# Keys once a tile, loop limits a step ahead, the count flag behind the maxima, two scrap rows and rotated banks in a graph network kernel

## The reference

```
# block 1: attention, residual
h   = layernorm(x) @ W1                       # 4 heads of 192
e   = leaky_relu(s_src[src] + s_dst[dst]); a = softmax of e over the edges of each dst
o1  = sum over edges of a * h[src] + b1       # then the same again with W2, 2 heads of 96 -> o2
x1  = layernorm(x + concat(x, o2) @ Wu + bu)
# block 2: graph convolution, residual
norm = deg^-0.5[src] * deg^-0.5[dst]          # self-loops included
y   = relu(segsum((x1 @ V1)[src] * norm) + c1)
out = layernorm(x1 + segsum((y @ V2)[src] * norm) + c2)
```

## Time and profile before

| | us |
|---|---|
| median of 3 runs | 895.5 |
| lowest, highest | 892.07, 897.51 |
| the profiled execution, device time | 891.93 |
| its span, first to last instruction | 890.2 |
| TensorE busy in it | 805.7 (91%) |
| VectorE busy | 612.3 (69%) |
| ScalarE busy | 287.3 (32%) |

### The profile page before, as it was taken

The page is one execution under the profiler, slowest core; times in us unless marked ns, Lnnn a source line. Parts: engine busy times, 40 slices in busy tenths (PEclk is TensorE's granted clock), DMA queues, the critical chain, the costliest instruction groups (busy, mean ns, idle before and its releaser), DMA issues.

```text
span 890.2 us, 12683 instructions
## 1 busy us (share of the span) xinstructions
PE 805.7 (91%) x4306; PEld 667.0 (75%) x4307; DVE 612.3 (69%) x1304; ACT 287.3 (32%) x523; POOL 18.7 (2%) x32
## 2 busy tenths in 40 slices
PE   4999999998899199999989879699998999999997
PEld 3845555655666099999955679478887888999997
DVE  1788888887738999999689799765641823212444
ACT  4334555543532143434232444322221411111000
POOL 3100000000000040000000000000000000000000
PEclk9999999999989699999989898799999999999999
DMA  8300000000000040110000400000003000000111
GB/s 290 138 1 1 1 0 0 0 0 1 1 0 1 7 172 1 60 60 1 1 1 0 134 1 1 2 1 1 1 0 126 1 1 1 1 1 1 54 71 50
DMA packets 9573, 26.34 MB, mean 30 GB/s; under 512 B 623, under 2 KB 2477, under 8 KB 9138
## 3 DMA queue, kind: packets, MB, share of 16 engines
q1 hardware_dynamic: 9522, 25.65, 8.3%
HBM read 21.78 MB, written 3.87 MB: 29 GB/s over the span
## 4 chain that ended last, share of the span: by engine, by line
PE 66%; DVE 19%; issue 5%; DVEq 5%; ACT 3%; DMA 1%; SPq 0%
PE ps L1059 63%; DVE scrap L510 5%; DVE att L662 3%; DVEq L319 3%; DVE att L626 3%; DVE ohs_abc L521 1%; DMA w<-in_L_gnn_W 1%; DVEq L521 1%; DVE ohd_ab L524 1%; DVE ohd_c L524 1%; PE ps L1198 1%; DVE xohd L524 1%; DVE out L649 1%; DVE gw1lo L702 1%; PE ps L1339 1%
## 5 line engine op out<-in xcount | busy, mean ns | idle before, releaser
L1059 PE MATMUL ps<-g,att 128*128 128x193 f32 x800 | 133.2, 330 | 19.8 <-DVE att L626 19.8
L1059 PEld LDWEIGHTS ps<-g,att 128*128 128x128 f32 x800 | 132.3, 192 | 20.8 <-issue 20.4
L931 ACT ACTIVATE att<-att,ssrc 128x1250 f32<-128x1250 f32 x60 | 80.2, 1338 | 116.1 <-DVE att L662 116.0
L626 DVE SCALAR_TENSOR_TENSOR att<-att,ct 128x1250 f32<-128x1250 f32 x60 | 88.0, 1467 | 4.8 <-ACT att L931 4.6
L662 DVE SCALAR_TENSOR_TENSOR att<-uB,s 128x1250 f32<-128x1250 f32 x60 | 91.1, 1522 | 0.0
L1059 PE MATMUL ps<-wp,xT 128*128 128x388 f32 x240 | 87.6, 503 | 0.9 <-ACT xT L878 0.6
L1059 PE MATMUL ps<-yhi,ctr 128*128 128x384 f32 x200 | 67.7, 339 | 0.0
L726 DVE SCALAR_TENSOR_TENSOR ylo_a<-ps,dinv,yhi 128x384 fp32r<-128x384 f32 x32 | 19.0, 615 | 61.9 <-ACT yhi L815 61.9
L1059 PEld LDWEIGHTS ps<-wp,xT 128*128 128x128 f32 x240 | 42.8, 191 | 24.6 <-issue 1.0
L1059 PE MATMUL ps<-h2x,att 128*128 128x97 f32 x400 | 51.8, 294 | 10.0 <-DVE out L649 4.6
L1059 PEld LDWEIGHTS ps<-h2x,att 128*128 128x128 f32 x400 | 50.4, 209 | 11.4 <-DVE att L626 8.0
(11 more groups left out here) (238 smaller groups left out, 1467.2 us busy)
## 6 DMA issues: line engine op xcount, KB each, us to landing
wux<-in_L_gnn_Wu SPq DMA_DIRECT2D x2, 2304.0 KB, 15.9
gw<-in_L_gnn_W SPq DMA_DIRECT2D x2, 2304.0 KB, 10.0
uB<-u_dram SPq DMA_DIRECT2D x3, 1280.0 KB, 5.9
xs<-in_x SPq DMA_DIRECT2D x1, 3456.0 KB
out<-ybuf SPq DMA_DIRECT2D x9, 384.0 KB, 2.3
w<-in_L_gnn_W SPq DMA_DIRECT2D x1, 2304.0 KB, 8.5
w2x<-in_L_gnn_W SPq DMA_DIRECT2D x1, 576.0 KB, 9.2
wuo<-in_L_gnn_Wu SPq DMA_DIRECT2D x1, 576.0 KB
```

What stands on the lines that cost most here:

```text
L626: v.scalar_tensor_tensor(a, a, HUGE, ct[:, q, 0:N], ALU.min, ALU.mult).then_inc(att_ready, 1)
L931: a.activation(at_, at_, ACT.Exp, bias=ssrc[:, h, q:q + 1]).then_inc(att_exp, 1)
L1059: return t.matmul(o, lhsT, rhs, start=start, stop=stop, **kw)
```

## The change

- **Key once a count tile.** `key` is made once a tile (relative to the tile's first column); three new tables vkey1, vkey2, vkey3, written once by POOL, hold the values of `vkey` moved by 32, 64 and 96, and window w compares with the w-th. The wait for the key stands once at the head of the tile.
- **Loop limits one step ahead.** The limits of a tile's first window are loaded at its head. Those of windows 1 to 3 are loaded during the window before: on VectorE `end` behind unit 0 and `unit0` behind unit 1, on TensorE `end` behind unit 1. `first` is the `end` of the window before and isn't loaded.
- **Two scrap rows.** Maxima write to two rows in turn and wait for the last but one.
- **Flag behind the maxima.** The 30 maxima of heads 1 to 3 stand ahead of the wait for `dmax_ps`, the flag and the reciprocals.
- **Rotated banks.** In layer 1 the five banks of a head rotate over seven (0 to 4, 6, 7); TensorE waits for a bank only from the eighth use on. Layer 2 stays with banks 0 to 4.

```diff
--- before.py
+++ after.py
@@ -166,6 +166,8 @@
         ssB_a = at("ssB_a", [P, H1 - 1, NP], F32, R_WP)
         ssB_d = at("ssB_d", [P, NP], F32, R_G)
         scrap1 = at("scrap1", [P, NP], BF16, R_WP + 15360)
+        scrap1b = at("scrap1b", [P, NP], BF16, R_T1 + 7680)
+        scrap2b = at("scrap2b", [P, NP], BF16, R_G + 14400)
         uRow = at("uRow", [VR, P], F32R, R_T1 + 12800)
         uLine = at("uLine", [2 * T, P], F32, R_T1 + 12800)
         o2T = at("o2T", [P, 2, H2, P], F32, R_WP + 9472)
@@ -180,6 +182,9 @@
         ohd_ab = at("ohd_ab", [P, 2, PR, WC, 2], BF16, R_T1 + 5120)
         xohd = at("xohd", [P, 2, PR, WC, 2], BF16, R_T1 + 10240)
         ohd_d = at("ohd_d", [P, PR, WC, 2], BF16, R_MASK + (T - 1) * NP * 2)
+        vkey1 = at("vkey1", [P, WC, 2], I16, R_T1 + 7680)
+        vkey2 = at("vkey2", [P, WC, 2], I16, R_T1 + 8960)
+        vkey3 = at("vkey3", [P, WC, 2], I16, R_T1 + 1536)
         sRow = at("sRow", [VR, P], F32R, R_T1 + 12288)
         h2x = at("h2x", [P, T, H2, C2 + 1], F32, R_T1)
         x1Thi = at("x1Thi", [P, KD, P], F32R, R_T1 + 6144)
@@ -273,6 +278,7 @@
         win_ps, win_out = sem("win_ps"), sem("win_out")
         ct_out = sem("ct_out")
         wu_plus = sem("wu_plus")
+        vkeys_set = sem("vkeys_set")
         xh_ready = sem("xh_ready")
         svec_hi = sem("svec_hi")
         tp_ps, tp_out = sem("tp_ps"), sem("tp_out")
@@ -340,6 +346,9 @@
         def src_row(hp):
 
             return ([ssB_a[:, h, :] for h in range(H1 - 1)] + [ssB_b[:, :], ssB_c[:, :], ssB_d[:, :]])[hp]
+
+        def acc_bank(hp, b):
+            return (0, 1, 2, 3, 4, 6, 7)[(5 * hp + b) % 7] if hp < H1 else b
 
         def wide_counts(eng):
 
@@ -426,6 +435,9 @@
             step(pool.iota(iota[:, :, :], pattern=[[1, P], [0, 2]], base=0, channel_multiplier=0, **io))
             pool.iota(wcol[:, :], pattern=[[W, NW]], base=0, channel_multiplier=0, **io).then_inc(const_a, 1)
 
+            pool.wait_ge(const_a, 1)
+            for w, table in enumerate((vkey1, vkey2, vkey3)):
+                pool.iota(table[:, :, :], pattern=[[NP, T], [1, W], [0, 2]], base=W * (w + 1), channel_multiplier=0, **io).then_inc(vkeys_set, 1)
             for wu, loaded in ((wux, wux_in), (wux2, wux2_in)):
                 pool.wait_ge(loaded, 16)
                 for k in range(KD):
@@ -505,47 +517,52 @@
 
             def maximum(h, q, done):
 
-                if done > 0:
-                    v.wait_ge(mx_done, done)
-                v.tensor_tensor_reduce(out=(scrap1 if h < H1 else scrap)[:, 0:N], in0=src_row(h)[:, 0:N], in1=mask[:, q, 0:N], scale=1.0, scalar=-FAR,
+                if done > 1:
+                    v.wait_ge(mx_done, done - 1)
+                place = ((scrap1, scrap1b) if h < H1 else (scrap, scrap2b))[done % 2]
+                v.tensor_tensor_reduce(out=place[:, 0:N], in0=src_row(h)[:, 0:N], in1=mask[:, q, 0:N], scale=1.0, scalar=-FAR,
                                        op0=ALU.subtract, op1=ALU.max, accum_out=mx[:, h % H1, q:q + 1]).then_inc(mx_done, 1)
 
-            def window(q, w):
+            def one_hots(p0, src_hot, dst_hot, vk, kv, done):
+                v.tensor_tensor(src_hot, iota[:, None, :, :].to_broadcast([P, PR, P, 2]), sloT[:, bass.ds(p0, PR), None, :].to_broadcast([P, PR, P, 2]), ALU.is_equal)
+                v.tensor_tensor(dst_hot, vk[:, None, :, :].to_broadcast([P, PR, WC, 2]), kv[:, bass.ds(p0, PR), None, :].to_broadcast([P, PR, WC, 2]), ALU.is_equal).then_inc(done, 1)
+
+            def window(q, r, w, limits):
+
                 win = WPT * q + w
-                first, end, unit0 = window_range(v, win, 0, 1, 2)
-
-                kv = key[:, w % 2, :, :].rearrange("p a c -> p (a c)")
-                v.tensor_scalar(kv, keyT[:, :, :].rearrange("p a c -> p (a c)"), wcol[:, bass.ds(win, 1)], None, ALU.subtract).then_inc(v_own, 1)
-
-                def one_hots(p0, src_hot, dst_hot, done):
-                    v.tensor_tensor(src_hot, iota[:, None, :, :].to_broadcast([P, PR, P, 2]), sloT[:, bass.ds(p0, PR), None, :].to_broadcast([P, PR, P, 2]), ALU.is_equal)
-                    if done is unit_ready:
-                        v.wait_ge(v_own, V0 + win + 1)
-                    v.tensor_tensor(dst_hot, vkey[:, None, :, :].to_broadcast([P, PR, WC, 2]), key[:, w % 2, bass.ds(p0, PR), None, :].to_broadcast([P, PR, WC, 2]), ALU.is_equal).then_inc(done, 1)
-
+                first, end, unit0 = limits
+                vk, kv = (vkey, vkey1, vkey2, vkey3)[w], key[:, r, :, :]
+                nxt = [end]
                 for j in range(UW):
                     slot = (UW * w + j) % RING
                     v.wait_ge(unit_used, UW * win + j + 1)
                     p0 = nc.s_assert_within(v.snap((unit0 + j) * PR), 0, (UN - 1) * PR,
                                             skip_runtime_bounds_check_because="the first unit was clamped")
-                    one_hots(p0, ring_src(slot), ring_dst(slot), unit_ready)
+                    one_hots(p0, ring_src(slot), ring_dst(slot), vk, kv, unit_ready)
+                    if w + 1 < WPT and j < 2:
+                        nxt += window_range(v, win + 1, j + 1)
                 with v.Fori(first, end) as n:
                     p0 = nc.s_assert_within(v.snap((unit0 + UW + n - first) * PR), 0, (UN - 1) * PR,
                                             skip_runtime_bounds_check_because="the range was clamped to the units")
                     place = v.snap(n % 2)
                     v.wait_ge(extra_used, n + 1)
-                    one_hots(p0, xohs[:, bass.ds(place, 1), :, :, :].rearrange("p a b v c -> p (a b) v c"), xohd[:, bass.ds(place, 1), :, :, :].rearrange("p a b v c -> p (a b) v c"), extra_ready)
-
-
-            def tile(q, behind, last):
-
-                window(q, 0)
+                    one_hots(p0, xohs[:, bass.ds(place, 1), :, :, :].rearrange("p a b v c -> p (a b) v c"), xohd[:, bass.ds(place, 1), :, :, :].rearrange("p a b v c -> p (a b) v c"),
+                             vk, kv, extra_ready)
+                return nxt
+
+            def tile(q, r, behind, last):
+
+                limits = window_range(v, WPT * q, 0, 1, 2)
+                v.tensor_scalar(key[:, r, :, :].rearrange("p a c -> p (a c)"), keyT[:, :, :].rearrange("p a c -> p (a c)"), wcol[:, bass.ds(WPT * q, 1)], None,
+                                ALU.subtract).then_inc(v_own, 1)
+                v.wait_ge(v_own, V0 + q + 1)
+                limits = window(q, r, 0, limits)
                 if behind:
                     dense_out(q - 1, 1)
-                window(q, 1)
+                limits = window(q, r, 1, limits)
                 if last:
                     dense_out(q, 0)
-                window(q, 2)
+                limits = window(q, r, 2, limits)
                 dense_out(q, 1 if last else 0)
                 if last:
                     v.wait_ge(dn_out, 2 * T + 2)
@@ -553,18 +570,19 @@
                     v.tensor_copy(svec[:, 0:H1 * T], a4).then_inc(svec_hi, 1)
                     v.wait_ge(svec_hi, 1)
                     v.tensor_tensor(svec[:, VLO:VLO + H1 * T], a4, svec[:, 0:H1 * T].bitcast(F32), ALU.subtract).then_inc(vec_ready, 1)
-                window(q, 3)
+                window(q, r, 3, limits)
 
 
             v.memset(svec[:, :].bitcast(F32), 0.0)
             v.memset(uvecs[:, :].bitcast(F32), 0.0)
             v.tensor_tensor(sel[:, :], identf[0:VR, 0:H1 * T], identf[0:VR, VLO:VR], ALU.add)
-            tile(0, False, False)
+            v.wait_ge(vkeys_set, WPT - 1)
+            tile(0, 0, False, False)
             with v.Fori(0, (T - 2) // 2) as i:
-                tile(2 * i + 1, True, False)
-                tile(2 * i + 2, True, False)
-            tile(T - 1, True, True)
-            n_own = [V0 + NW]
+                tile(2 * i + 1, 1, True, False)
+                tile(2 * i + 2, 0, True, False)
+            tile(T - 1, 1, True, True)
+            n_own = [V0 + T]
 
             def vstep(ins):
                 n_own[0] += 1
@@ -607,14 +625,14 @@
             vstep(v.tensor_reduce(deg[:, :], degp[:, :, :], AX.X, ALU.add))
             v.sem_inc(deg_ready, 1)
             v.tensor_reduce(degmax[:, :], deg[:, :], AX.X, ALU.max).then_inc(dmax_ready, 1)
+            for h in range(1, H1):
+                maxima(h)
             v.wait_ge(dmax_ps, 1)
             vstep(v.tensor_reduce(zz[0:1, 0:1], ps[0:1, 5, 0:P], AX.X, ALU.max))
             v.tensor_scalar(wide[0:1, 0:1], zz[0:1, 0:1], float(EXACT), None, ALU.is_gt).then_inc(wide_ready, 1)
             v.wait_ge(sq_ready, 1)
             vstep(v.reciprocal(dinv[:, :], sqd[:, :]))
             v.tensor_tensor(dinv2[:, :], dinv[:, :], dinv[:, :], ALU.mult).then_inc(dinv_ready, 1)
-            for h in range(1, H1):
-                maxima(h)
             v.wait_ge(x_added, 2 * X2)
 
 
@@ -633,7 +651,7 @@
                         v.wait_ge(acc_ps, 4 * hp + b + 1)
                     else:
                         v.wait_ge(att_used, T * (hp + 1))
```

(18 more changed lines are left out.)

## The result

| | before | after |
|---|---|---|
| median, us | 892.1 (10 runs) | 885.5 (10 runs) |
| ratio to before, 95% interval | | 0.9926 (0.9908 to 0.9945) |
| span of the profiled execution, us | 890.2 | 883.1 |

The change gains 6.6 us, where 26.2 were forecast; 885.5 lies above the predicted range. One of the two terms came as forecast, and the other came with the wrong sign. Lines of the kernel after lie some lines further down: the one-hots are 527 and 528 (521 and 524 before), the maxima 523 (510), ScalarE's copy 833 (815), the first operation of attention 680 (662).

The account below looks back on a forecast made before the run. TensorE's matmul line held 63% of the chain; time could come from the count stage (44 to 224 us) and 243 to 312 us. 12 + 14.2 = 26.2 us, so 895.5 - 26.2 = 869.3; own range 865 to 873, whole range 861 to 879.

Parts of the forecast that it names:

- Term B: Flag behind the maxima, between count stage and attention: line 662 starts at 293.1 instead of 307.31, 14.2 us gained.
- What is late next: Ahead of line 662, once the maxima start earlier: ScalarE's last copy of line 618, at 292.47 for 0.49 us.
- The maxima's pace of 1.47 us: VectorE's 30 maxima of heads 1 to 3 with two scrap rows: 1.47 us apart, 44.1 us in all.
- Scrap rows 0: Second scrap row for VectorE's maxima: worth nothing in either layer, since line 618's copy ends later than the maxima.
- banks 0: Rotated banks in layer 1's heads: worth 0, since TensorE is busy 128.00 of 128 us there.
- POOL's additions at the head of attention: POOL's 9.11 us of additions to wux2, now in attention's first tiles, slowing VectorE's operations: charged 0, bound 1.5 us.
- The rival that set 3.3 us on it: POOL's additions starve TensorE at attention's head and its slow clock lasts longer: B = 10.9, 872.6 us; chance 0.10.
- Term A: Count stage, key once a tile and limits a step ahead: 12 us gained, bounds 5 and 15.5.
- the change doesn't do what it says: Rival, count stage: loads stall inside the window as they did between; A = 0, 881.3 us, chance 0.03.
- 15.71 us for a tile with one extra unit a window: TensorE's least time for a count-stage tile, from 4.14 + 4.61 + 3.48 + 3.48.
- what I left for waiting: Part of the eight loop tiles' 13.5 us of waiting for one-hots taken to remain: 0.4 a tile, 3 in all.
- TensorE's floor of 127.1: TensorE's least time for the count stage's eight loop tiles, 8 x 15.71 + 5 x 0.28 = 127.1 us.

Follow-up runs that it names:

- b_flag: Kernel before with one edit, the maxima of heads 1 to 3 ahead of the wait for the flag of wide counts: 878.9 us, ratio 0.9848.
- b_pad128: Kernel before with 128 semaphore increments that nothing waits for ahead of VectorE's program: 892.8 us, ratio 1.0012.
- b_pad72: Kernel before with 72 semaphore increments that nothing waits for ahead of VectorE's program: 902.5 us, ratio 1.0122.
- a_pad3: Changed kernel with 3 semaphore increments that nothing waits for ahead of VectorE's program: 889.1 us in a single run.
- a_pad8: Changed kernel with 8 semaphore increments that nothing waits for ahead of VectorE's program: 868.8 us, ratio 0.9728.

## Why the prediction was wrong, point by point

- **Term B, 14.2 us: right.** By the stretch from the last window to the first operation of attention it is 14.2, by the runs of b_flag 13.3. What is late next was right as well: ScalarE's copy. The maxima's pace of 1.47 us was wrong (1.38), and so was their start (2.1 us earlier than I had it); neither mattered, since that copy sets the end.
- **Scrap rows 0, banks 0: right**, by a run each. What the prediction did not see is that the scrap rows' zero depends on term B: without it they are worth 0.24 x 30 = 7 us (83.6 against 76.2 us in the two profiles).
- **POOL's additions at the head of attention, charged 0: right.** They start at 306.09 and stretch VectorE's operations there to 1.71 us, but TensorE's only wait for VectorE in layer 1's heads is the first, 5.9 us. From line 680 to the first attention matmul it is 5.17 us and not 4.91, 0.3 more, and the heads take 132.8 us as before. The rival that set 3.3 us on it is out.
- **Term A, 12 us: the step that failed.** I counted what VectorE executes and what its queue issues, instruction by instruction, and took for granted that the instructions are there. That the edit takes some out ahead of the loop and out of its body was in the sum only as time saved, not as a move of the loop's code. Its price is the three slow rounds: 151.3 - 132.9 = 18.5 us in the loop. None of my rivals had it; "the change doesn't do what it says" was the nearest, at 881.3, with another mechanism. The trace of before had the sign at hand: no instruction packet between 93 and 197 us, though VectorE runs over 300 instructions a round there, so its loop lived on what the engine holds.
- **What term A is without that:** with 8 increments the count stage ends at 214.85 instead of 223.68: 8.8 us, not 12. The loop gives 7.7 (132.9 against 140.6) where I had 10.5, the last tile 1.3, the first nothing. The working was right in kind. I had 15.71 us for a tile with one extra unit a window; the one that closes at 128.13 takes 15.84, with 3.48 in both last windows. The term that was mis-sized is what I left for waiting: of the 13.5 us above TensorE's floor of 127.1 I kept 3, and 5.8 stayed. They lie in three places. The tile's 15.84 against 15.71 makes 1.0. The five windows with a second extra unit are longer than the same window with one by 4.1 together, where I priced the unit at its two matmuls, 0.28, 1.4 for the five. Two of them are 0.3 longer, as priced; the other three are 1.0 to 1.3 longer, and in these TensorE stands still in front of the unit's matmuls, waiting for VectorE's second pair (0.44, 0.44 and 0.37 us by name). That leaves 2.7 on top of the price. The window from 128.13 to 133.52 is one of the three, 5.39 us against 4.13, and took 5.44 in the kernel before. Near its end stands:

```profile
133.02 0.47 PE L1081 MATMUL ps<-xohd,xohs 128*128 x2 [0.44 <-DVE xohd L532]
```

  The last 2.1 are in other windows, most of them the first of a tile, where VectorE has the loads and the key at the tile's head in front of it.
- **The whole sum.** The kernel with its loop on the right side takes 868.8 us against the 869.3 forecast for the changed one. That is partly luck: 3.2 us too much in term A are set off against the median of before, which came out at 892.1 in the longer series and not at 895.5. The gain is 23.3 us, the forecast was 26.2.

The account of the changed kernel is then: -8.8 for the count stage as it can be, -14.2 for the turn, +19.8 for the placement (the last window closes at 234.67 and not at 214.85), -4.7 for the faster turn between the layers in its profile: -7.9, against a span that fell by 7.1.

The Trainium skill (Runtime: NRT & Kernel Launch, section "Instruction fetch mechanics") says that instructions are prefetched in order only, and that a taken branch whose target isn't in what the engine holds waits for a DMA fetch. The trace agrees: two stops of 2.1 and 1.9 us behind the branch at 95 us, and 5.1 to 5.5 us of idle on VectorE behind each of the three. It gives two blocks of 16 KB for most engines; here VectorE's packets are 8 KB and a body over three of them ran without a fetch, and the measurement decides.

**A version that beats both kernels** is the changed one with eight instructions that do nothing ahead of the loop: 868.8 us, 2.7% under before. Five gave 865.0 in a single run.

## What to carry to other kernels

A loop that an engine repeats has an address. When an edit changes the number of instructions ahead of a hot loop or in it, look at the packets of that engine's instruction queue inside the loop, before and after: none should be there. If they appear and the engine is idle with "issue" behind the back branch, move the code by a few instructions and time it again before judging the edit. And terms that shorten two sides of one wait don't add: test the second with the first in place and without it.

## What the runs showed of the hardware

- VectorE's code is fetched in 8 KB packets, and a period of 128 instructions fits the effect of its place (b_pad128 equals before, b_pad72 doesn't). A body over four of these blocks cost 5 fetches a round (15 packets for three rounds, in after and in b_pad72). The queue stopped twice behind the back branch, VectorE was idle there for 4 to 5.6 us (b_pad72, after, a_pad3), and with TensorE's low clock behind the pause the changed kernel lost some 6 us a round. On q8, which I take for TensorE's instruction queue though no run tests it, the packets are 16 KB (32 in 0.52 MB). The page of a_pad8:

```profile
q8 instruction: 32, 0.52, 0.3%
q14 instruction: 18, 0.15, 0.1%
```

- Two maxima in a row on VectorE with different scrap rows start 1.38 us apart though each is shown with 1.46: the ends overlap. With one row, and so a wait on the one before, they are 1.61 us apart.
